# A graph network on one core: the count matrix as the moving operand, in pairs of blocks

## The reference, cut to what matters

```python
x = _layernorm(x + L0(x))   # 4 layers: attention sums, rmsnorms, a hidden product
x = _layernorm(x + L1(x))   # softmax over the edges of a node, weighted sum of x[src]
x = _layernorm(x + L2(x))   # two graph convolutions
x = _layernorm(x + L3(x))   # segment_sum(x[src] * edge_weight, dst)

def _graph_conv(h, src, dst, n, W_root, W_rel, b):
    agg = segment_sum(h[src], dst, num_segments=n)
    return h @ W_root.T + agg @ W_rel.T + b
h   = relu(_graph_conv(x, src, dst, n, W1_root, W1_rel, b1))
out = relu(_graph_conv(h, src, dst, n, W2_root, W2_rel, b2))
```

## Time and profile before

| | |
|---|---|
| median of 3 runs | 4938.74 us |
| lowest, highest | 4912.16, 4939.90 us |
| the profiled execution, its own time | 4902.4 us |
| its span | 4900.6 us |
| mean granted clock of TensorE | 0.887 |
| PE, PEld busy | 3921.1, 3185.6 us |
| DVE, ACT, POOL busy | 3512.9, 2093.4, 905.6 us |
| DMA | 404.97 MB, mean 83 GB/s |

### The profile page before, as it was taken

The page is one execution under the profiler, slowest core; times in us unless marked ns, Lnnn a source line. Parts: engine busy times, 40 slices in busy tenths (PEclk is TensorE's granted clock), DMA queues, the critical chain, the costliest instruction groups (busy, mean ns, idle before and its releaser), DMA issues.

```text
span 4900.6 us, 236239 instructions
## 1 busy us (share of the span) xinstructions
PE 3921.1 (80%) x108223; PEld 3185.6 (65%) x108223; DVE 3512.9 (72%) x4267; ACT 2093.4 (43%) x2437; POOL 905.6 (18%) x809
## 2 busy tenths in 40 slices
PE   5532957859368588888888886999999799999997
PEld 4531856848358466666666665997898566666665
DVE  5875676877758877777777766553554699999997
ACT  5201112010010477767667764662564245544453
POOL 0565757534422410000000000000000000000000
PEclk9975786959669799999999998997999699999998
DMA  6751443616225111111111113552553000000000
GB/s 159 246 142 30 117 139 84 183 58 174 63 63 171 47 53 54 53 54 53 47 54 53 54 51 100 178 179 79 171 177 125 5 10 11 10 10 11 10 11 17
DMA packets 208019, 404.97 MB, mean 83 GB/s; under 512 B 106418, under 2 KB 126132, under 8 KB 207268
## 3 DMA queue, kind: packets, MB, share of 16 engines
q1 hardware_dynamic: 181672, 383.04, 24.9%
q0 software_dynamic: 25472, 10.79, 1.1%
q10 hardware_dynamic: 184, 0.08, 0.0%
HBM read 287.83 MB, written 110.03 MB: 81 GB/s over the span
## 4 chain that ended last, share of the span: by engine, by line
PE 69%; DVE 11%; issue 7%; POOL 3%; ACT 3%; DMA 1%; DVEq 0%; ACTq 0%; SPq 0%
PE psum L1110 19%; PE psum L1083 15%; PE psum L1150 13%; PE psum L910 10%; PE psum L1071 4%; POOL heads_d L602 2%; PE psum L878 2%; POOL gath L610 1%; DVE space L1637 1%; PE psum L991 1%; PE psum L992 1%; PE psum L852 1%; ACT space L759 1%; PE psum L1159 1%; DVE space L1422 1%
## 5 line engine op out<-in xcount | busy, mean ns | idle before, releaser
L764 ACT COPY space<-psum 128x784 f32<-128x784 f32 x1184 | 966.1, 816 | 627.4 <-PE psum L1083 625.4
L1083 PE MATMUL psum<-space 64*128 64x49 bf16 x56832 | 986.7, 184 | 179.1 <-issue 149.1
L1083 PEld LDWEIGHTS psum<-space 64*128 64x128 bf16 x56832 | 851.6, 94 | 389.2 <-issue 279.1
L1110 PE MATMUL psum<-space,X 128*64 128x256 f32 x7252 | 1039.2, 396 | 14.8 <-issue 12.2
L1637 DVE TENSOR_TENSOR space<-space 128x2352 bf16<-128x2352 bf16 x592 | 814.3, 1376 | 0.0
L910 PE MATMUL psum<-table,space 128*128 128x56 bf16 x24300 | 674.8, 189 | 118.7 <-DVE space L1292 77.8
L910 PEld LDWEIGHTS psum<-table,space 128*128 128x128 fp8e4 x24300 | 660.7, 96 | 132.8 <-issue 116.6
L1631 DVE TENSOR_TENSOR space<-space,V 128x2048 bf16<-128x2048 bf16 x592 | 720.9, 1218 | 0.0
L1150 PE MATMUL psum<-space 128*128 128x192 bf16 x7252 | 627.3, 247 | 23.8 <-DVE space L1733 23.8
L1150 PEld LDWEIGHTS psum<-space 128*128 128x128 bf16 x7252 | 593.9, 98 | 49.4 <-issue 48.8
L1289 DVE TENSOR_REDUCE space<-psum 128x1512 f32 (+1 forms) x300 | 518.5, 1731 | 137.5 <-PE psum L910 132.6
(11 more groups left out here) (284 smaller groups left out, 2892.8 us busy)
## 6 DMA issues: line engine op xcount, KB each, us to landing
space<-adj_d SPq DMA_DIRECT2D x148, 784.0 KB, 4.2
space<-onehots SPq DMA_DIRECT2D x240, 432.0 KB
adj_d<-space SPq DMA_DIRECT2D x74, 784.0 KB, 3.6
onehots<-space SPq DMA_DIRECT2D x60, 432.0 KB, 3.2
space<-digit_rows SPq DMA_DIRECT2D x60, 378.0 KB
space<-cw_d SPq DMA_DIRECT2D x37, 160.0 KB, 2.3
cw_d<-space SPq DMA_DIRECT2D x4, 1184.0 KB, 13.3
heads_d<-spread,heads_at POOLq DMA_INDIRECT x280
```

What stands on the lines that cost most here:

```text
L764: nc.scalar.copy(A[:, h, :, b * P:(b + 1) * P].rearrange("p a (w s) -> p w a s", w=2)[:, :, :, c:c + UC], psum[:, 2 + 2 * (k % 2):4 + 2 * ...
L1083: mm = nc.tensor.matmul(psum[:, 2 + 2 * (k % 2) + w, c * NB:(c + 1) * NB], ohlo[lo:hi, ring, col // 2, :, col % 2], ohw[lo:hi, ring, r, co ...
L1110: mm = nc.tensor.matmul(pb[6][half:half + F, 0:2 * P], X[:, a, :], A[:, 1 - h, a, :], start=(a < 2), stop=(a >= NB - 2))
```

## The change

The stored counts are applied pair by pair with the operands exchanged: a piece of the features (64 columns) is stationary, and the counts of both blocks of the pair (256 columns) move. The result has features in partitions, even slices in the lower half and odd ones in the upper. So per pair ACT copies it from PSUM (`turned_sum`), PE folds the halves and turns it (`fold_sum`), ACT copies again (`slots3`), and PE places both blocks (`place_slots`), here into PSUM partitions 64 to 127, as acc now lies in xT[64:128]. The product with the weights then is one matmul of 128 rows, and the bias is added by DVE. The cast writes the two blocks side by side, in four parts a pair, two on ACT (22 slices) and two on DVE (27). The first two pairs are loaded and cast earlier, acc is zeroed by POOL, and a block's counts are stored in four DMAs, each at a later unit.

```diff
+STORES = [(0, 13), (13, 25), (25, 37), (37, NB)]
-HALF = (NB // 2 + 1) * P
+CUTS = [(0, 12), (12, 22), (22, 36), (36, NB)]
...
+        adj8 = view(0, 2 * 2 * NB * P // 4, U8).rearrange("p (h b a s) -> p h b a s", h=2, b=2, s=P)
+        counts = view(at, 2 * NB * P, BF16).rearrange("p (h a s) -> p h a s", h=2, s=2 * P)
...
+            def store_counts(i, h, b, last=False):
+                for q, (lo, hi) in enumerate(STORES):
+                    sp.wait_ge(adj_made, i * (4 * GU) + ((2 * h + b + 1) * GU + (0 if last else q)))
...
+                    sp.dma_start(adj_d[at, :, lo * P:hi * P].rearrange("b p x -> (b p) x"),
+                                 adj[:, b, lo:hi, :].rearrange("p a s -> p (a s)")).then_inc(adj_stored[b], 16)
...
             def pair(n, i, h, more=True):
                 if n == 0:
-                    for b in range(2):
...
+                    store_counts(i, h, 0)
                 if more:
                     sp.wait_ge(hot_ready, i * (2 * HS) + (n * NDB * HS + (h + 1) * HS))
...
+                if n == 0:
+                    store_counts(i, h, 1, isinstance(i, int) and 2 * i + h == NDB - 1)
...
+            first_loads(0)
             sp.wait_ge(x_ready, 2 * LAYERS + 3)
             sp.dma_start(x_d.rearrange("(j p) f -> p j f", p=P), X[:, :, :]).then_inc(x_stored, 16)
             apply_loads(0)
+            first_loads(1)
...
-            nc.gpsimd.memset(xT[F:F + 1, :], 1.0).then_inc(ones_back, 1)
+            nc.gpsimd.memset(xT[F:P, :], 0.0).then_inc(acc_zero, 1)
+            pool.wait_ge(mm_psum, NMG)
+            nc.gpsimd.memset(xT[F:P, :], 0.0).then_inc(acc_zero, 1)
...
+            def cast(n, i, h, parts=(0, 1)):          # ACT
+                d = i * 2 + (n * NDB + h)
+                act.wait_ge(adj_loaded[h], i * 32 + 32 * (n * (NDB // 2 + 1 - h) + 1))
+                for g in parts:
+                    lo, hi = CUTS[g]
+                    if not isinstance(i, int) or i:
+                        act.wait_ge(applied, d * 4 + (g + 1 - 8))
...
+                    nc.scalar.copy(counts[:, h, lo:hi, :].rearrange("p a (b s) -> p b a s", b=2), adj8[:, h, :, lo:hi, :]).then_inc(cast_act, 1)
+            def apply_step(n, i, h, at):
...
+                    nc.scalar.copy(turned_sum[:, 1 - h, :], pb[1 - h][:, 0:2 * P]).then_inc(row_ready, 1)
...
+                    nc.scalar.copy(slots3[:, h, :, :], pb[2 + h][:, 0:2 * F].rearrange("p (b f) -> p b f", b=2)).then_inc(slots_out, 1)
...
-                        nc.tensor.matmul(o, xT[0:F + 1, j * P:(j + 1) * P], weights, start=True, stop=False)
-                        mm = nc.tensor.matmul(o, acc[0:F, j * P:(j + 1) * P], more, start=False, stop=True)
+                        mm = nc.tensor.matmul(o, xT[:, j * P:(j + 1) * P], bothT[:, n, :], start=True, stop=True)
...
+            def apply_step(n, i, h, at):              # PE
+                D = i * 2 + (n * NDB + h)
+                if at < NDB:
+                    if n or at >= 2:
+                        pe.wait_ge(row_ready, D - 1)
+                    for g, (lo, hi) in enumerate(CUTS):
+                        pe.wait_ge(cast_act if g < 2 else cast_dve, D * 2 + (g % 2 + 1))
+                        for a2 in range(lo, hi, 2):
+                            for k in range(3):
+                                for a in range(a2, min(a2 + 2, hi)):
+                                    half = F * (a % 2)
+                                    mm = nc.tensor.matmul(pb[h][half:half + F, 0:2 * P], pieces[:, k, a * F:(a + 1) * F], counts[:, h, a, :],
+                                                          start=(a < 2 and k == 0), stop=(a >= NB - 2 and k == 2))
+                        mm.then_inc(applied, 1)
+                        if g == 1 and at >= 2:
+                            place_slots(D, h, at)
+                        if g == 2 and at >= 1:
+                            fold_sum(D, h, at)
...
+            def place_slots(D, h, at):
+                pe.wait_ge(slots_out, D - 1)
+                pe.wait_ge(place_ready, D - 1)
...
+                for b in range(2):
+                    mm = nc.tensor.matmul(pb[4 + h][F:P, b * P:(b + 1) * P], slots3[:, h, b, :], place[:, h, b, :], start=True, stop=True)
+            def fold_sum(D, h, at):
+                pe.wait_ge(row_ready, D)
...
+                for b in range(2):
+                    mm = nc.tensor.matmul(pb[3 - h][:, b * F:(b + 1) * F], turned_sum[:, 1 - h, b * P:(b + 1) * P], fold[:, :], start=True, stop=True)
...
+            def apply_step(n, i, h, at, bases):       # DVE: merge two windows, write two one-hots, cast
...
+                        win = xT[F:P, bass.ds(bases[b], WIN)]
+                        nc.vector.tensor_tensor(win, pb[5 - h][F:P, b * P:(b + 1) * P], win, ALU.add).then_inc(merged, 1)
...
-                link(nc.vector.memset(acc, 0.0))
+                dve.wait_ge(acc_zero, n + 1)
...
+            cast(0, 0, 0)
+            cast(0, 0, 1)
             for u in (1, 2):
                 blocks(u - 1)
+                if u == 1:
+                    cast(1, 0, 0)
+                    cast(1, 0, 1)
...
+                    nc.vector.tensor_tensor(x, p, biases[:, u - 1, :].unsqueeze(1).to_broadcast([P, hi - lo, F]), ALU.add).then_inc(mm_read, 1)
```

More of the change, by code:

```diff
@@ L788, in _ @@
             weighted_sum(0)
[L789 to L797, removed]
-            for n in range(2):
+            square(0, NB)
@@ L800, in _ @@
+            cast(0, 0, 0, parts=(0,))
+            root(0, NB)
+            cast(0, 0, 0, parts=(1,))
+            for n in range(2):
+                if n:
+                    cast(n, 0, 0)
+                    cast(n, 0, 1)
+                else:
+                    for h in range(2):
+                        act.wait_ge(adj_stored[h], 16 * len(STORES) * NDB)
+                copy_xt(0, NB)
                 if n == 0:
+                    cast(n, 0, 1)
+                for at in range(4):
+                    apply_step(n, at // 2, at % 2, at)
+                with act.Fori(2, NDB // 2) as i:
@@ L982, in carries, with products @@
                 carry_column(n, back)
-            def products(n, weights, more):
+            def products(n):
                 for g in range(NMG):
@@ L1172, in acc_rows @@
+                for at in range(NDB - 1, NDB + 2):
+                    apply_step(n, at // 2, at % 2, at)
             def acc_rows(n):
@@ new lines, in cast @@
+            def cast(n, i, h):
+                d = i * 2 + (n * NDB + h)
+                dve.wait_ge(adj_loaded[h], i * 32 + 32 * (n * (NDB // 2 + 1 - h) + 1))
+                for g in (2, 3):
+                    lo, hi = CUTS[g]
+                    if not isinstance(i, int) or i:
+                        dve.wait_ge(applied, d * 4 + (g + 1 - 8))
+                    elif n:
+                        dve.wait_ge(applied, 4 * NDB)
+                    nc.vector.tensor_copy(counts[:, h, lo:hi, :].rearrange("p a (b s) -> p b a s", b=2), adj8[:, h, :, lo:hi, :]).then_inc(cast_dve, 1)
@@ new lines, in apply_step @@
+            def apply_step(n, i, h, at, bases):
+                D = i * 2 + (n * NDB + h)
+                if at >= 3:
+                    dve.wait_ge(placed, D - 2)
+                    for b in range(2):
+                        win = xT[F:P, bass.ds(bases[b], WIN)]
+                        nc.vector.tensor_tensor(win, pb[5 - h][F:P, b * P:(b + 1) * P], win, ALU.add).then_inc(merged, 1)
+                        dve.wait_ge(merged, D * 2 + (b + 1 - 6))
+                if 1 <= at <= NDB:
+                    if at >= 3:
+                        dve.wait_ge(placed, D - 2)
+                    for b in range(2):
+                        block = bass.ds(i * 4 + (2 * h - 2 + b), 1) if not isinstance(i, int) else slice(4 * i + 2 * h - 2 + b, 4 * i + 2 * h - 1 + b)
+                        ins = nc.vector.tensor_scalar(place[:, 1 - h, b, :], iota_row[:, :], slot_rel[:, block], None, ALU.is_equal)
+                    ins.then_inc(place_ready, 1)
+                if 1 <= at < NDB - 1:
+                    cast(n, i + h, 1 - h)
@@ L1751, in blocks, with bases_at @@
+            def bases_at(first, count):
+                return nc.values_load_multi_w_load_instructions(slot_base[0:1, first:first + count] if isinstance(first, int) else slot_base[0:1, bass.ds(first, count)],
+                                                                engines=[mybir.EngineType.DVE], min_val=0, max_val=N - 1)[1]
             def blocks(n):
```

195 lines of the change are left out of this document (91 added, 104 removed).

## The result

| | before | after |
|---|---|---|
| median, first comparison | 4939.9 us | 4809.11 us (4792.29 to 4817.81, 5 runs) |
| ratio | | 0.9747, 95% interval 0.9708 to 0.9785 |
| repeated on another occasion | 4926.91 | 4813.63, ratio 0.9766 (0.9750 to 0.9782) |
| profiled execution | 4902.4, span 4900.6 | 4792.29, span 4790.5 |

Forecast were 4885 us and a range of 4835 to 4940. The sign was right, the gain was twice what was forecast, and the time lies outside the range. One of the five executions of the kernel before in the first comparison took 10597 us and is left out of the ratio. Windows of the changed kernel by stage, columns as in rows 1: the first weighted sum, the first apply loop with its end, products() with DVE's part, the second apply loop.

What follows compares the result with a forecast made beforehand. PE's time per instruction was taken to bound the apply loops and products(). Loops +29, products() −75, loop starts −8.6 and +1, loop ends +1.5 summed to −52 us; from the median, 4885 us, range 4835 to 4940.

Steps and rivals of the forecast that it cites:

- Weighted sum. … Cost nothing; bounds 0 and … +11: Weighted sum: 74 stores become 296 quarters, at no cost; +11 us if each pair's first ACT copy waited 0.3 us.
- Placing … 0.46 taken; at best nothing: Apply loops, once a pair: four f32 placing instructions cost 0.46 us, or nothing if the other half goes on beside them.
- +0.39 us a pair: Apply loops: a pair takes 9.41 us instead of 9.02, +29 us over 74 pairs.
- The slot of 109.5 ns: Apply loops: two bf16 matmuls on different halves stream together in 109.5 ns; 75 slots, 8.21 us a pair.
- the fold's 0.74: Apply loops, once a pair: folding 0.59 us, array running empty 0.10, getting going 0.05, together 0.74 us.
- (a): Rival, apply loops: half-array weight loads are not hidden in bf16, +178 us, 5065 us; chance 0.12.
- (b): Rival, apply loops: the halves do not overlap in bf16, 16.2 us a pair, 5480 us; chance 0.03.
- The rule that a changed tiling mode drains the array: Apply loops: by the skill's rule the fold pays twice a pair and placing nothing; a step costs about 0.1 us.
- 0.446 us a call: products(): 49 calls with K = 128 at 0.446 us each instead of 98 alternating K = 65 and 64; 21.9 us.
- (d): Rival, products(): the clock stays up, 11 us each, −22 us more, 4863 us; chance 0.12.
- Memset goes to POOL, which is idle: Start of the second loop: the 5.4 us memset leaves DVE for POOL, part of the −8.6 us there.
- −8.6 and +1: Loop starts: −8.6 us at the second (memset and casts moved away), +1 us at the first.

Runs made afterwards that it cites:

- before_four: The kernel before with only the stores changed: four per block, each one unit later, the second block's behind the load of cw; ratios 0.9952 and 0.9958.
- extra_stores: The kernel before with 74 more DMAs of 784 KB, one per block, in the second weighted sum; 4949.72 us, ratio 1.0068.
- swap_halves: The changed kernel with even slices in the upper half, odd in the lower, so the partnerless slice shares the placing's half; 9.33 us a pair, ratio 0.9876.
- halves apart: The changed kernel with all even slices of each group first, then all odd ones; 14.34 us a pair, 5199.93 us, ratio 1.0555.
- threes: The changed kernel with three matmuls of an even slice, then three of its odd neighbour, instead of one by one; 9.25 us a pair.

## Why the prediction was wrong

- **"Weighted sum. … Cost nothing; bounds 0 and … +11"** failed: the stage came 36 us shorter in the profiles. I asked only whether the store lands before its buffer is written again, and who waits on its semaphore. The cost of the old store was elsewhere: PE's instruction packets stand behind it, and PE idles in "issue" gaps, 150 us of them in this stage, 124 after. They were not among my rows. before_four shows 24 to 26 us of the whole time for the stores alone, and extra_stores 27 us for large stores where there were none. The rest, some 9 us, goes for the most part with the granted clock of the two profiles compared, which is luck.
- **"Placing … 0.46 taken; at best nothing"** failed, and with it +0.39 us a pair. I priced it by L1098, which writes the same half as the L1110 matmul behind it, and took that for the price of a placing that writes the other half. It takes one slot: the lower half has 75, the upper 72 + 4 = 76. 76 × 0.109 + 0.74 = 9.02 us, measured 9.03 to 9.04 (and 4.52 us a block before, by rows 4, so 9.04 for two). My lower bound, "placing free", was the truth, and stood in the range; the loops moved by under 1 us each, not +14.5. swap_halves shows the mechanism.
- **The slot of 109.5 ns**, from L1110 in f32, held in bf16 (2 × 54.9), and the fold's 0.74 with it. Rivals (a) and (b) fall: loads of the half array are hidden, and the halves overlap. The rule that a changed tiling mode drains the array (the Trainium skill, "TensorEngine Tiling (Array Packing)", Key Properties) was to make the fold pay and placing nothing. The trace agrees: the sum with a fold of 0.74 comes out, 0.21 us lie between the starts of the fold's last matmul and the next count matmul (3210.87, 3211.08) where the slot is 0.109, and the placing fits between the count matmuls with no step.
- **products()**: 0.446 us a call was foretold, 3.42 us for eight calls, 0.427, came, at the lower clock (0.50 granted in that stretch); (d), a clock that stays up, did not happen. The 37.5 us were the right size. The sum missed that "Memset goes to POOL, which is idle" is not free: 3 to 5 us between the loops. The cover was idle, but not independent of DVE.
- **Start of the loops**: −8.6 and +1 against −8.7 (21.2 to 12.5) and +1.0.
- **The range** took the lower bound of each priced term (4831). It held none for a term called nothing, and none below zero for the weighted sum, though the stores there were changed in size, number and time.

## What to carry to other kernels

A large DMA that nobody waits for can still cost an engine that works through many instructions, as these come by DMA too: look at that engine's "issue" gaps and at the instruction queue's packets, and spread the bytes over time rather than only cutting them. With a half-width stationary operand, count slots for each half of the array, alternate the halves from one matmul to the next, and put small extra matmuls on the half with fewer; f32 calls in a row should have the same number of rows. An engine that is idle may share a path with a busy one: place its memsets where the other waits.

## What the runs showed of the hardware that I had not expected

- Matmuls of different halves of the PSUM partitions start out of program order, by up to three matmuls (three counts between four placements; 14.34 us a pair with the halves apart, 9.25 with threes, 9.03 alternating).
- A relu of 0.43 us on DVE took 5.37 us beside a GpSimd memset of 5.43 us, and 0.88 beside one of 0.95: it ends 0.3 us behind the memset.
- In a stage bound by PE all "issue" gaps over 0.5 us (127 before, 125 after) end 1.15 to 1.65 us behind an instruction packet of 16 KB, and such packets hardly start in the first three microseconds behind a store of 784 KB.
- Alternating K = 65 and K = 64 costs 0.19 us on each call (0.617 against 0.427) at 1.2 GHz; 65 rows in every call cost nothing like it (0.446).
- 74 stores of 784 KB that nothing waits for lengthened a stage bound by PE by 23 to 30 us (1014.5 against 984.8 to 991.4); the same bytes in quarters, spread, by 2 to 9 (993.8).
